# A graph network's edge stage: source numbers by batch, row writes between the batches, and the edge bias written into the banks by ScalarE

## The reference, cut to what matters

```python
# 6250 nodes of 256 numbers, 206250 edges sorted by dst
# layer 0: agg = segment_sum(concat(x[src], edge_attr_64) @ W_message, dst)
h = layer_norm(relu(agg) + x); nodes_out = relu_mlp_skip(h, 3 layers)
x1 = layernorm(x + layer_norm(x + nodes_out))
# layer 1: attention over neighbours
h = lrelu(x1 @ w_W + w_b)
edge_h = lrelu(edge_attr_128 @ ew_W + ew_b)
e_ij = concat([h[tgt], h[nbr], edge_h], -1) @ a_W + a_b
alpha = segment_softmax(e_ij, tgt)
x = layernorm(x1 + lrelu(segment_sum(alpha * h[nbr], tgt)))
```

## Time and profile before

| | |
|---|---|
| median of three runs | 6130.2 us |
| profiled execution | 6137.35 us |
| its span | 6135.6 us |
| TensorE busy | 4380.8 us (71%) |
| VectorE busy | 3925.9 us (64%) |
| GpSimd busy | 3605.0 us (59%) |
| ScalarE busy | 1625.7 us (26%) |
| mean granted TensorE clock | 0.872 |

### The profile page before, as it was taken

One profiled execution on the slowest core, in us unless ns is written; L12 is line 12 of the kernel. 1 busy time (PEld: TensorE's weight loads), 2 busy tenths in 40 slices (PEclk: granted clock), 3 DMA queues, 4 the chain that ended last, 5 costly groups with the idle time before them and its releaser, 6 DMA issues. The chain is left out here.

```text
span 6135.6 us, 96444 instructions
## 1 busy us (share of the span) xinstructions
PE 4380.8 (71%) x20840; PEld 3144.9 (51%) x20841; DVE 3925.9 (64%) x11948; ACT 1625.7 (26%) x4443; POOL 3605.0 (59%) x3679
## 2 busy tenths in 40 slices
PE   5477777778777777787887773676666677767662
PEld 3255555555555555555555542555555555555552
DVE  8666665666666666666665654666666666666665
ACT  0011111111111111111111111444444444444444
POOL 0354555555555555555555441777777777777774
PEclk9698998998899989988899886888888888888886
DMA  1344444444444444444444462444444444444442
GB/s 38 98 126 113 130 126 121 119 131 121 117 120 130 124 116 120 132 124 116 124 128 126 112 109 86 104 106 106 105 105 105 105 105 105 105 105 104 103 106 77
DMA packets 573021, 682.69 MB, mean 111 GB/s; under 512 B 368278, under 2 KB 404462, under 8 KB 572732
## 3 DMA queue, kind: packets, MB, share of 16 engines
q0 software_dynamic: 175296, 472.19, 29.6%
q1 hardware_dynamic: 382716, 196.39, 12.3%
q10 hardware_dynamic: 14976, 13.69, 0.6%
HBM read 653.36 MB, written 27.66 MB: 111 GB/s over the span
## 5 line engine op out<-in xcount | busy, mean ns | idle before, releaser
L610 POOL DMA_INDIRECT rows<-in_x,picked x1785 | 1785.7, 1000 | 1533.3 <-DVE picked L1006 1004.0
L1453 POOL DMA_INDIRECT nbr<-nodetab,nbr_idx x1760 | 1665.9, 947 | 593.7 <-issue 526.9
L642 PE MATMUL bank<-w_edge,feats 128*128 128x258 f32 x3264 | 1064.7, 412 | 778.4 <-DVE unused L998 716.1
L1483 PE MATMUL bank<-nbr,w 128*128 128x258 f32 x3520 | 1133.6, 477 | 192.3 <-ACT w L1529 191.9
L657 PE MATMUL bank<-rows,hot 128*128 128x320 f32 x3570 | 1254.1, 451 | 10.3 <-DMA rows<-in_x,picked 5.7
L642 PEld LDWEIGHTS bank<-w_edge,feats 128*128 128x128 f32 x3264 | 574.9, 201 | 1017.9 <-DVE unused L998 820.8
L1483 PEld LDWEIGHTS bank<-nbr,w 128*128 128x128 f32 x3520 | 775.8, 231 | 429.5 <-ACT w L1529 299.2
L1515 ACT ACTIVATE w<-off,logit 128x128 f32<-128x128 bf16 x1760 | 562.1, 390 | 1184.8 <-DVE logit L1568 1117.2
L998 DVE SCALAR_TENSOR_TENSOR unused<-bank,a_relu 128x258 bf16<-128x258 f32 x1632 | 682.4, 422 | 169.6 <-PE bank L643 145.4
L657 PEld LDWEIGHTS bank<-rows,hot 128*128 128x128 f32 x3570 | 592.6, 199 | 259.7 <-issue 49.0
L1474 PE MATMUL bank<-ident,w 128*128 128x128 f32 x1760 | 311.5, 304 | 501.3 <-ACT w L1515 499.3
(11 more groups left out here) (316 smaller groups left out, 5340.1 us busy)
## 6 DMA issues: line engine op xcount, KB each, us to landing
feats<-in_edge SPq DMA_DIRECT2D x408, 256.0 KB, 3.4
rows<-in_edge SPq DMA_DIRECT2D x255, 128.0 KB, 2.9
rows<-in_x,picked POOLq DMA_INDIRECT x1785, 2.8
nbr<-nodetab,nbr_idx POOLq DMA_INDIRECT x1760, 2.8
rows<-in_edge SPq DMA_DIRECT2D x153, 160.0 KB, 3.7
nbr_idx<-nbr_all SPq DMA_DIRECT2D x440, 2.0 KB
nodetab<-tab ACTq DMA_DIRECT2D x52, 129.0 KB
x_blk<-in_x SPq DMA_DIRECT2D x52, 128.0 KB
```

The lines of the kernel that those rows point to most:

```text
L610: pool.indirect_dma_start(out=rows[:, s, 0:D], out_offset=None, in_=a["x"], in_offset=bass.IndirectOffsetOnAxis(ap=picked[h][:, s:s + 1].b ...
L642: mm(y, feats[:, f0 * P:(f0 + 1) * P], w_edge[:], start=True, stop=False)
L1453: pool.indirect_dma_start(out=nbr[:, u * GC + k, :], out_offset=None, in_=nodetab, in_offset=bass.IndirectOffsetOnAxis(ap=nbr_idx[u][:, k: ...
L1483: ins = mm(O_PS[u % 2][:, 0:HW], w[:, u * GC + k, :], nbr[:, u * GC + k, :], start=(k == 0), stop=(k == GC - 1))
```

## The change

`picked` becomes eight buffers, one for each batch, each copied by VectorE one step behind the step in which the next batch starts (8, 12, 16, 19, 22, 25, 28), the last at step 31. GpSimd runs batch 0, the first write, batches 1 and 2, the second write, batches 3 to 7. The positions are copied at steps 21 and 29. The bias product of each tile goes. In its place ScalarE copies `b_edge` (128 x 258, float32) into the tile's bank two steps ahead (seed), behind VectorE's reading of the bank four tiles before; TensorE's one product adds onto it (`start=False`) and waits at even steps for the seeds of both tiles of the pair. Four products ahead of the passes mark the banks as written. VectorE's chain for the bias parts goes.

```diff
-            b_parts = sb("b_parts", [P, D + 2], BF16, ctx)
+            b_edge = sb("b_edge", [P, D + 2], F32, ctx)
-            picked = [sb(f"picked{h}", [P, SA], I32, ctx) for h in range(2)]
+            picked = [sb(f"picked{j}", [P, max(SUMS)], I32, ctx) for j in range(NB_SUMS)]
...
-                def gathers(p, h):
-                    wait_alone(pool, (o["picked_ready"], p * 2 + (h + 1)))
-                    for j in range(*HALVES[h]):
-                        wait_alone(pool, (o["summed"], p * NB_SUMS + (j + 1)))
-                        for s in range(STARTS[j], STARTS[j] + SUMS[j]):
+                def gathers(p, *batches):
+                    for j in batches:
+                        wait_alone(pool, (o["picked_ready"], p * NB_SUMS + (j + 1)), (o["summed"], p * NB_SUMS + (j + 1)))
+                        for s in range(SUMS[j]):
                             pool.indirect_dma_start(
-                                out=rows[:, s, 0:D], out_offset=None, in_=a["x"],
-                                in_offset=bass.IndirectOffsetOnAxis(ap=picked[h][:, s:s + 1].bitcast(U32), axis=0),
+                                out=rows[:, STARTS[j] + s, 0:D], out_offset=None, in_=a["x"],
+                                in_offset=bass.IndirectOffsetOnAxis(ap=picked[j][:, s:s + 1].bitcast(U32), axis=0),
                             ).then_inc(x_in[j], 16)
...
                     gathers(p, 0)
                     write(p, 0)
-                    gathers(p, 1)
+                    gathers(p, 1, 2)
                     write(p, 1)
+                    gathers(p, 3, 4, 5, 6, 7)
...
                     if kk % 2 == 0:
-                        pe.wait_ge(o["logit_ready"], p * TILES + (kk - EB + 2 + LOG0))
+                        pe.wait_ge(o["seeded"], p * TILES + (kk + 2))
...
-                    mm(y, feats[:, f0 * P:(f0 + 1) * P], w_edge[:], start=True, stop=False)
-                    mm(y, ones_bf[:], b_parts[:], start=False, stop=True).then_inc(o["y_ready"], 1)
+                    mm(y, feats[:, f0 * P:(f0 + 1) * P], w_edge[:], start=False, stop=True, skip_group_check=True
+                       ).then_inc(o["y_ready"], 1)
...
+                for b in range(EB):
+                    ins = mm(banks[b][:, 0:D + 2], ones[:], w_edge[:], start=True, stop=True)
+                ins.then_inc(o["primed"], 1)
...
+                AHEAD = 2
+                def seed(p, kk):
+                    act.wait_ge(o["logit_ready"], p * TILES + (kk - EB + 1 + LOG0))
+                    s.copy(banks[kk % EB][:, 0:D + 2], b_edge[:]).then_inc(o["seeded"], 1)
...
                 def body(p):
                     for kk in range(TILES):
+                        seed(p, kk + AHEAD)
...
+                act.wait_ge(o["primed"], 1)
+                for kk in range(AHEAD):
+                    seed(0, kk)
...
-                link(v.memset(b_parts[:], 0.0))
-                for n in range(3):
-                    link(v.tensor_copy(part_bf, b_edge))
-                    link(v.tensor_copy(part_f, part_bf))
-                    link(v.tensor_tensor(b_edge, b_edge, part_f, ALU.subtract))
-                    link(v.tensor_scalar(rstd[:], lane[:, 0:1], float(n), None, ALU.is_equal))
-                    link(v.scalar_tensor_tensor(b_parts[:], part_f, rstd[:, 0:1], b_parts[:], ALU.mult, ALU.add))
...
-                def pick(p, h, tile):
+                def pick(p, j, tile):
                     if not isinstance(p, int):
-                        dve.wait_ge(o["summed"], p * NB_SUMS + HALVES[h][1])
-                    a0, a1 = STARTS[HALVES[h][0]], STARTS[HALVES[h][1]] if h == 0 else SA
-                    v.tensor_copy(picked[h][:, a0:a1], src_i[:, bass.ds(tile + a0, a1 - a0)]).then_inc(o["picked_ready"], 1)
+                        dve.wait_ge(o["summed"], p * NB_SUMS + (j + 1))
+                    v.tensor_copy(picked[j][:, 0:SUMS[j]], src_i[:, bass.ds(tile + STARTS[j], SUMS[j])]).then_inc(o["picked_ready"], 1)
...
+                pick_at = {(SUM_KK[j + 1] + 1 if j + 1 < NB_SUMS else TILES - 1): j for j in range(NB_SUMS)}
...
-                        if kk in (8, 9):
-                            place(p, kk - 8, e)
+                        if kk in (21, 29):
+                            place(p, (21, 29).index(kk), e)
...
-                        if kk == 19:
-                            pick(p + 1, 0, tile)
+                        if kk in pick_at:
+                            pick(p + 1, pick_at[kk], tile)
...
-                        if kk == 31:
-                            pick(p + 1, 1, tile)
```

More of the change, by code:

```diff
@@ L520, in build @@
                 "slot_ready", "tagged_ready", "sorted", "rows_ready", "at_ready", "summed", "hot_ready",
-                "picked_ready", "tot_ready", "base_ready", "rel_ready", "go_ready", "keys_ready", "folded", "packed", "turned", "parts_ready")}
+                "picked_ready", "tot_ready", "base_ready", "rel_ready", "go_ready", "keys_ready", "folded", "packed", "turned", "parts_ready", "seeded", "primed")}
             rows_out = sem("rows_out", ctx)
@@ L537, in build @@
             SUM_AT = [FIRST + s * (LAST - FIRST + 1) // SA for s in range(SA)]
-            HALVES = ((0, 4), (4, NB_SUMS))
             def count_of(eng):
@@ L866, in _ @@
                 flat = "p t n -> p (t n)"
-                junk, part_f = hot[0][:].rearrange(flat)[:, 0:D], hot[0][:].rearrange(flat)[:, 0:D + 2]
-                b_edge = hot[1][:].rearrange(flat)[:, 0:D + 2]
-                part_bf = unused[:, 0, :]
+                junk = hot[0][:].rearrange(flat)[:, 0:D]
                 link(v.memset(tab[:], 1.0))
@@ L1161, in _ @@
                 tile = tile_at(dve, 0)
-                pick(0, 0, tile)
-                pick(0, 1, tile)
+                for j in range(NB_SUMS):
+                    pick(0, j, tile)
                 base_of(0)
```

## The result

The changed kernel takes 5615.5 us (median of four runs, 5608.9 to 5616.85) against 6135.1 us for the kernel before in the same comparison: a ratio of 0.915, with an interval of 0.9132 to 0.9168. A later set on a chip of the same speed gave 5619.2 against 6137.2 us, 0.9153 (0.9137 to 0.9168). The forecast was 5630 us.

The account below looks back on a forecast made before the run. The prediction took GpSimd and VectorE waiting for each other in turns to set the 68.1 us pass. Its terms gave 58.3 us, 9.8 less, times 51 passes = 500 us off 6130: 5630 us, range 5490 to 5830.

Parts of the forecast that it names:

- The ring: GpSimd and VectorE wait in turns, 68.1 us a pass; ending VectorE's 15.70 us place wait gains 11.65.
- 4.05 of the wait stay under other names: Part of VectorE's place wait that remains, at step 11, for the MLP's first activation.
- tile 8: TensorE's tile at step 6 waits for its seed behind the copies of `hb`, starting 1.15 us later.
- No new ring through step 21: GpSimd waits at the first write for step 21's position, but stays covered while a pass exceeds 48.3 us.
- Seeds: ScalarE's bias copies, 0.4 us each; 1.15 lost at step 6 less 0.4 for dropped products: 0.75 us a pass.
- The table load: ScalarE's 1.28 us load delays seeds 2 and 3 at steps 0 and 1; covered, 0 us, at most 2.0.
- Behind the scan: TensorE runs ahead after the scan, so the last residual's layer wait goes: 0.9 us gained, between 0 and 1.7.
- The clock: TensorE's half-speed phases: 1.3 us a pass at the message product, plus new ones at seeds' stops; 1.5 in all.
- Rival 2: A half-speed phase behind each of two new TensorE stops, 2.4 us each: 61.6 us a pass, 5800 us, chance 0.15.
- The sum: All terms of a pass together: 68.1 - 11.65 + 0.75 - 0.9 + 0.5 + 1.5 = 58.3 us.
- 1 and 5: Whole place wait goes, 5330 us, chance 0.07; the wait cycle holds through step 21, 6130 us, chance 0.02.
- 3 and 4: Seeds on the path at every pair, 5930 us, chance 0.08; slower through many half-speed phases, 6530 us, chance 0.04.

Follow-up runs that it names:

- order alone: Kernel before with source numbers by batch, writes between batches and late positions; bias product kept, no seeds: 5583.9 us, ratio 0.9098 to the kernel before.
- idle products: Changed kernel plus 44 unused 128-column products at TensorE's steps 1 and 23, in its two long stops: 5494.9 us, ratio 0.8953 to the kernel before.
- seed 9 first: Changed kernel with ScalarE's seed 9 issued at step 6 ahead of the copies of `hb`, not behind: 5615.2 us, ratio 0.9152 to the kernel before.

## Why the prediction was right, point by point

- *The ring*: right. 15.70 us of waiting became 5.57, and the step "4.05 of the wait stay under other names" was 1.5 us too small. With the order alone, in the pass from 1158.22, the same stretch waits 0.65 + 1.43 + 0.39 + 2.19 = 4.66 us, so 0.6 of the 1.5 belong to the ring and 0.9 to the late tile 8, which the sum had as a term of its own. The remainder was expected in front of one residual, about 5 us; only 2.19 stand there.
- *No new ring through step 21*: right. GpSimd waits up to 6.0 us for the position, and TensorE waited for rows once, 4.0 us.
- *Seeds*: tile 8 as forecast (a wait of 1.26 for 1.15, worth 1.11 us by the split passes), and the copy takes 0.38 us, forecast 0.4. But the net price of 0.75 us a pass is wrong: at a clock of 1.00 it is nothing. The sum gave back 0.4 for the products left out; the runs give back all of it, 0.67 of it behind the scan. That the whole difference between the two kernels is 0.85, near the forecast 0.75, is luck: it is made by the clock (1.0 us more a pass in the changed kernel).
- *The table load*: seed 2 started at 1026.57 behind a load that ended at 1026.56, so nothing stands between them. The Trainium skill, "ScalarE: Activation LUTs", section "What ACT_TABLE_LOAD costs", has a drain of about 1.38 us there; this row disagrees as the earlier trace rows did.
- *Behind the scan*: from the scan to the last residual it is 1059.40 - 1049.64 = 9.76 us, before 1149.98 - 1138.66 = 11.32. 1.56 gained, 0.9 forecast; inside the bounds. With the order alone it is 1168.65 - 1158.22 = 10.43, 0.89 gained, as forecast, and 0.67 come with the seeds. In that kernel the last residual still waits for its layer:

```profile
1168.65 0.43 DVE L1065 TENSOR_TENSOR h_t<-h_t,s_t 128x256 f32<-128x256 f32 x1 [0.88 <-ACT s_t L805]
```

- *The clock*: the mis-sized term, and the one with the wrong working. I took 1.5 us a pass, the idle products show 2.4. Of the 1.5, 1.3 were for the message product behind a slow phase; that wait is 1.2 us at most in the changed kernel, so this part did not come. The 0.2 left for new phases at the seeds' stops were in fact 1.54 + 1.03 us. The stops were the right ones (before tiles 2 and 24). The Trainium skill, "TensorE: Matmul & The Clock Gate", Part 1, takes the low clock for the default that activity lifts, and the trace agrees in part: in the changed kernel both stops have their phase in the pass, and with products in the stops the clock is 1.00, but in order alone the same stops of 2.56 and 1.65 us come with a phase in some passes and without one in others. Rival 2 put two phases at 2 x 2.4 = 4.8 us; they cost half of that.
- *The sum*: without the clock 56.8 us were forecast and 55.76 measured, with it 58.3 and 58.17. Two errors, 1.0 too much and 0.9 too little, cancel, so the nearness of 5630 to 5615.5 is in part luck. Of the first error 0.9 is the price of the seeds (0.75 forecast, -0.12 by the two passes at a clock of 1.00); the rest was not parted.
- *Rivals*: 1 and 5 fall by the wait lists, 3 and 4 by the 0.85 us between the changed kernel and order alone. That the seeds lower the gain stood in the sum; that they do so through the clock alone did not. The better version at this speed is the order alone, and better still the changed kernel with idle products.

Open are: which part of the order ends the place wait at the speed of the result, and what late positions and writes between batches are worth there (the kernels that have them undone ran only on the slow chips); how much seed 9 first gives in time at a steady clock; what decides whether the clock falls behind a stop; why instructions come late on two of the chips.

## What to carry to other kernels

When two engines wait for each other in a ring, move the earliest hand-over forward (here the numbers of one batch, from step 19 to step 8, together with the order of writes and positions; the three were not parted at this speed). The long wait at the other end goes by itself, and what the next arrival leaves of it can be read off the trace beforehand. A stop of TensorE can be paid a second time, as slow products behind it: here two stops of 3.8 and 4.0 us cost 1.54 and 1.03 us a pass in that way. So moving a product to a free engine can lose (0.6% here) though it costs nothing at a steady clock, because it lengthens the stops, and filling the stops can win more (2.2%). Compare whole passes that have the same granted clock before putting a price on an edit. Before keeping such filling, run it on more than one chip: it gained 2.2% on one, and on another, where TensorE's instructions came late, a kernel with it was 1.9% slower than the kernel before. And read a wait list beside that of a kernel known to have the wait: on the slow chips the place wait was missing in the old order too.

## What the runs showed of the hardware that was not expected

GpSimd's issue of a gather takes 0.95 us, but beside VectorE's scan it took four times as long (3.95 to 4.23 us in each of ten passes). Beside VectorE's operation of 2.29 us behind it a gather took 2.88 us in order alone, where it starts inside the operation, and 0.95 in the changed kernel, where it starts 0.2 us ahead of it. Timeline of GpSimd in the changed kernel; the scan runs from 1049.64 for 3.62 us:

```profile
1048.81 0.95 POOL L608 DMA_INDIRECT rows<-in_x,picked  x1 [0.30 <-issue]
1050.06 3.96 POOL L608 DMA_INDIRECT rows<-in_x,picked  x1 [0.30 <-issue]
1054.33 1.70 POOL L608 DMA_INDIRECT rows<-in_x,picked  x1 [0.31 <-issue]
```

Before, GpSimd stood idle during the scan (19.91 us until 1155.22, with the scan from 1138.66); now it gathers there, and its mean issue is 1117 ns. TensorE waited for gathered rows once, so this is under cover. Three more are told above: the slow hand-out of TensorE's instructions (2.1 us for one, in stretches of more than 20 us); the slow phase that grew from 3.4 to some 6 us behind a stop of the same length; and passes of one kernel with the same stops that last 55.57, 57.22 or 58.62 us, at a clock of 1.00, 0.97 or 0.94 in that order.
